# Cutting the helpers' dependent pairs in two: moving small normalization and scaling operations between VectorE, GpSimd and ScalarE in a two-layer transformer kernel

## The reference

```python
# layer 0: linear attention, 8 heads of 32
xn = ln(x, ln_w, ln_b)
q = softmax(heads(xn @ Wq + bq), axis=-1)                        # over the 32 features of a head
k = softmax(heads(xn @ Wk + bk + (1 - mask) * -1e6), axis=1)     # over the tokens
v = heads((xn @ Wv + bv) * mask)
y = einsum('bnhd,bhdl->bnhl', q, einsum('bnhd,bnhl->bhdl', k, v))
scale, shift = split(silu(emb) @ W_emb + b_emb, 2)
x = x + silu(ln(y) * (1 + scale) + shift) @ W_out + b_out
# layer 1: full attention, 16 heads of 16
xn = ln(x, norm_w, norm_b)
att = softmax(einsum('bnhl,bmhl->bnmh', q, k) + (1 - mask) * -1e6, axis=2)
y = einsum('bnmh,bmhl->bnhl', att, v)
x = x + silu(ln(y) * (1 + scale) + shift) @ out_w + out_b
```

## Time and profile before

| | us | share of the span |
|---|---|---|
| median of three runs | 870.1 | |
| span of the profiled execution | 869.6 | |
| PE busy | 825.9 | 95% |
| DVE busy | 786.1 | 90% |
| POOL busy | 732.7 | 84% |
| ACT busy | 709.8 | 82% |
| PE weight loads busy | 590.2 | 68% |

### The profile page before, as it was taken

The page is one execution under the profiler, slowest core; times in us unless marked ns, Lnnn a source line. Parts: engine busy times, 40 slices in busy tenths (PEclk is TensorE's granted clock), DMA queues, the critical chain, the costliest instruction groups (busy, mean ns, idle before and its releaser), DMA issues.

```text
span 869.6 us, 25205 instructions
## 1 busy us (share of the span) xinstructions
PE 825.9 (95%) x8653; PEld 590.2 (68%) x8653; DVE 786.1 (90%) x1610; ACT 709.8 (82%) x1250; POOL 732.7 (84%) x1214
## 2 busy tenths in 40 slices
PE   9998788999999999999999999999999999999885
PEld 4487666677777777777677777777777776656443
DVE  6898899999999999999999999999998999998962
ACT  6457847897889798888888888888888788998794
POOL 6769999799999989989999999988998887887314
PEclk8899989999999999999999999999999999999998
DMA  8221464435352525343534434334453333444311
GB/s 224 77 38 40 118 109 103 105 76 116 98 134 56 143 76 105 90 121 100 125 97 82 132 86 111 91 103 114 85 130 106 78 84 85 112 123 103 103 31 37
DMA packets 149306, 85.84 MB, mean 99 GB/s; under 512 B 87478, under 2 KB 141852, under 8 KB 149180
## 3 DMA queue, kind: packets, MB, share of 16 engines
q1 hardware_dynamic: 149180, 84.23, 39.5%
HBM read 39.52 MB, written 25.79 MB: 75 GB/s over the span
## 4 chain that ended last, share of the span: by engine, by line
PE 47%; POOL 18%; DVE 15%; issue 10%; ACT 4%; DMA 3%; SPq 2%; POOLq 0%; DVEq 0%; ACTq 0%
PE banks L690 12%; PE banks L837 7%; DVE NM L1274 6%; PE banks L698 5%; PE banks L824 4%; PE banks L813 4%; PE banks L705 3%; POOL Z L1933 2%; PE banks L720 2%; POOL ZHL L1940 2%; PE banks L847 2%; DVE st L1175 2%; POOL AB L2004 2%; PE banks L756 2%; POOL ZHL L1937 2%
## 5 line engine op out<-in xcount | busy, mean ns | idle before, releaser
L1274 DVE TENSOR_REDUCE NM<-banks 128x4 f32<-128x1024 f32 x256 | 302.5, 1212 | 9.5 <-PE banks L813 8.4
L1696 ACT ACTIVATE wraw<-banks,uu 128x1024 f32<-128x1024 f32 x154 | 170.2, 1136 | 22.3 <-PE banks L824 21.4
L1696 ACT ACTIVATE PX<-banks,uu 128x1024 f32<-128x1024 f32 x102 | 113.6, 1138 | 14.5 <-PE banks L824 12.8
L690 PE MATMUL banks<-wo,SH 128*128 128x256 f16 x768 | 96.1, 277 | 7.6 <-POOL SH L1978 7.2
L1920 POOL TENSOR_TENSOR rs<-ve,nhalf 128x2 f32<-128x2 f32 x128 | 90.2, 705 | 10.6
L813 PE MATMUL banks<-SK,SQ 51*128 51x256 f16 x1024 | 88.8, 273 | 7.0 <-DVE NM L1274 3.1
L824 PE MATMUL banks<-SQ,SK 53*128 53x256 f16 x1024 | 88.4, 272 | 6.9 <-DVE NM L1274 2.0
L690 PE MATMUL banks<-wv,ZT 128*128 128x256 f16 x768 | 94.5, 273 | 0.3 <-DVE AT L1224 0.2
L1978 POOL TENSOR_TENSOR SH<-ST,SH 128x512 f16<-128x512 f32 x64 | 74.3, 1168 | 22.9 <-ACT SH L1664 22.9
L690 PEld LDWEIGHTS banks<-wo,SH 128*128 128x128 f16 x768 | 73.2, 99 | 24.4 <-POOL SH L1978 10.5
L1678 ACT ACTIVATE R<-banks,fcs,sqs 128x256 f32<-128x256 f32 x128 | 73.8, 577 | 19.4 <-PE banks L698 19.2
(11 more groups left out here) (187 smaller groups left out, 1925.2 us busy)
## 6 DMA issues: line engine op xcount, KB each, us to landing
scr<-AB SPq DMA_DIRECT2D x64, 256.0 KB, 2.5
X<-in_x_dram SPq DMA_DIRECT2D x32, 256.0 KB, 2.9
SQ<-scr SPq DMA_DIRECT2D x64, 128.0 KB, 2.7
SK<-scr SPq DMA_DIRECT2D x64, 128.0 KB, 2.8
out_dram<-wemb SPq DMA_DIRECT2D x32, 256.0 KB, 2.5
SQ<-scr SPq DMA_DIRECT2D x64, 64.0 KB, 2.8
SK<-scr SPq DMA_DIRECT2D x64, 64.0 KB, 2.8
wemb<-in_L_cond_emb_w_dram SPq DMA_DIRECT2D x1, 1024.0 KB, 5.3
```

Source lines behind the costliest of these rows:

```text
L690: m = PE.matmul(dst[:, t, :], zt[:, j, k, t * P:(t + 1) * P], w[:, i, k, :], start=(k, n) == (0, 0), stop=(k, n) == (1, 2))
L1274: V.tensor_reduce(NMe[:, c, :, 2 * g:2 * g + 2], banks[:, n:n + 2, :].rearrange("p a (h m) -> p a h m", m=T), AX.X, ALU.max, negate=True). ...
L1696: A.activation(px(v % 5), banks[:, n:n + 2, :].rearrange("p a n -> p (a n)"), ACT.Exp, scale=uu[:, 0:1]).then_inc(S["exp"])
```

## The change

The code of five pieces and a helper is cut, and three operations change their engine:

- `stats` keeps BN_STATS; BN_AGGR is a piece of its own on DVE, `a0` to `a3`.
- `nm` and `ve` are made on ScalarE (pieces `n0` to `n3`, two ACTIVATE of 128x2); `ve` has two buffers, and epsilon comes from a tile `epa`. `norm` on POOL keeps only the power.
- `parts` on POOL is three pieces: `c0`/`c1` (Z, now one pair of buffers for each layer), `h0`/`h1` (the high part) and `z0`/`z1` (the rest).
- `km` keeps the reduction on DVE, into a new tile `kmr`; its scaling is the piece `kn` on POOL.
- `rq` is `qd` (the sum) and `rq` (the reciprocal), `Y1_` is `rd_` and `Y1_`, both on DVE.
- Of `np_` the first half is the piece `nh` on POOL, the second stays on DVE.
- `mb3` and `mh3`, used in the setup, lie in PX2.
- The order lists of all five engines and the tables of PSUM banks are new throughout.

```diff
             def stats(b, l, src):
-                e.wait_ge(S[f"s{l}"], b)
+                e.wait_ge(S[f"a{l}"], b)
                 for t in range(2):
                     i = V.bn_stats(st[:, l, t, :], src[:, t, :])
-                follow(i)
+                i.then_inc(S[f"s{l}"])
+
+            def moments(b, l):
+
+                e.wait_ge(S[f"s{l}"], b + 1)
+                e.wait_ge(S[f"n{l}"], up(b - 1))
                 for t in range(2):
                     i = V.bn_aggr(mv[:, b % 2, l, t, :], st[:, l, t, :])
-                i.then_inc(S[f"s{l}"])
+                i.then_inc(S[f"a{l}"])
...
             def km(b):
                 e.wait_ge(S["k0"], b + 1)
-                e.wait_ge(S["ke"], b)
-                follow(V.tensor_reduce(kmx[:, :], bank(home("gk0", b)), AX.X, ALU.max, negate=True))
-                V.tensor_scalar(kmx[:, :], kmx[:, :], un[:, 1:2], None, ALU.mult).then_inc(S["km"])
+                e.wait_ge(S["kn"], b)
+                V.tensor_reduce(kmr[:, :], bank(home("gk0", b)), AX.X, ALU.max, negate=True).then_inc(S["km"])
...
             def np_(b):
-                e.wait_ge(S["max"], 8 * b + 8)
-                if b == 0:
-                    ready(e, "nmz")
-                else:
-                    e.wait_ge(d_nt[(b - 1) % 2], 16 * ((b - 1) // 2 + 1))
-                follow(V.tensor_scalar(NMp[:, :, 0, :], NM[:, :, :], 2.0 ** -15, None, ALU.mult))
+                e.wait_ge(S["nh"], b + 1)
                 V.scalar_tensor_tensor(out=NMp[:, :, 1, :], in0=NM[:, :, :], scalar=2.0 ** -15, in1=NMp[:, :, 0, :],
                                        op0=ALU.mult, op1=ALU.subtract).then_inc(S["np"])
...
         @block.scalar
         def _(e):
+            def mean_of(b, l):
+                k, a = l % 2, (ZS ** -2, 1.0)[l % 2]
+                e.wait_ge(S[f"a{l}"], b + 1)
+                e.wait_ge(S[("c0", "yn0", "c1", "yn1")[l]], up(b - 1))
+                first(e, b, "cst")
+                A.activation(nm[:, b % 2, l, :], mv[:, b % 2, l, :, 0], ACT.Copy, scale=-1.0)
+                A.activation(ve[:, b % 2, l, :], mv[:, b % 2, l, :, 1], ACT.Identity, bias=epa[:, k:k + 1],
+                             scale=a).then_inc(S[f"n{l}"])
...
             def norm(b, l):
 
-                a = (1.0, ZS ** -2)[l % 2 == 0]
-                e.wait_ge(S[f"r{l}"], b)
-                G.tensor_scalar(nm[:, b % 2, l, :], mv[:, b % 2, l, :, 0], -1.0, 0.0, ALU.mult, ALU.add)
-                follow(G.tensor_scalar(ve[:, l, :], mv[:, b % 2, l, :, 1], a, EPS * a, ALU.mult, ALU.add))
-                G.tensor_tensor(rs[:, b % 2, l, :], ve[:, l, :], nhalf[:, :], ALU.pow).then_inc(S[f"r{l}"])
+                e.wait_ge(S[f"n{l}"], b + 1)
+                e.wait_ge(S[("c0", "yn0", "c1", "yn1")[l]], up(b - 1))
+                G.tensor_tensor(rs[:, b % 2, l, :], ve[:, b % 2, l, :], nhalf[:, :], ALU.pow).then_inc(S[f"r{l}"])
...
+            def kn(b):
+                first(e, b, "w0p")
+                e.wait_ge(S["km"], b + 1)
+                e.wait_ge(S["ke"], b)
+                G.tensor_scalar(kmx[:, :], kmr[:, :], un[:, 1:2], 1.0, ALU.mult, ALU.mult).then_inc(S["kn"])
+
+            def nh(b):
+                e.wait_ge(S["max"], 8 * b + 8)
+                if b == 0:
+                    ready(e, "nmz")
+                else:
+                    e.wait_ge(d_nt[(b - 1) % 2], 16 * ((b - 1) // 2 + 1))
+                G.tensor_scalar(NMp[:, :, 0, :], NM[:, :, :], 2.0 ** -15, 1.0, ALU.mult, ALU.mult).then_inc(S["nh"])
...
-            cst(); r0(0); r0(1); z0(0); xb0(0); xb0(1); z0(1); pb(); pd(); r0(2); r0(3); z0(2); r0(4); nmz()
+            nmz(); cst(); r0(0); c0(0); r0(1); xb0(0); h0(0); z0(0); xb0(1); c0(1); h0(1); v1z(); r0(2); pb()
```

More of the change, by code:

```diff
@@ new lines @@
+    "gt_f0": "0",
+    "gv0": "46774347475362375043566521644326",
+    "ga_f0": "0",
+    "gbb2": "1",
+    "gkt": "24421567564736100556121060526771",
+    "gqt": "63666246647202446535500465360633",
+    "gat": "26442553076275567624414317153465",
+    "gy0": "26434727742675112073374333472601",
+    "grw": "5",
+    "gy0T": "43275242062527252124720722610466",
+    "gcol": "5",
+    "go0": "72376515371077472233160736640061",
+    "gt_b": "0",
+    "ga_o1": "1",
+    "gt_f1": "3",
+    "ga_b": "0",
@@ L108 @@
-    "gv0": (
-        "f1m ke:1 q1:2 q1:4 mx_b th0:3 max:9 kt:7 exp:6 Y1:2 th1:2 qa:7 x1:9 max:56 max:64 exp:61 q1:17 th0:15 "
-        "th0:16 x1:16 qt:20 x1:18 th0:20 th0:21 x1:21 x1:22 th0:24 max:168 max:176 x1:26 exp:182 ka:27 "),
+    "ghot": "-",
+    "gt_w0": "-",
+    "gcnd": "hot",
+    "gpm": "-",
+    "gt_w1": "-",
+    "gt_o0": "-",
+    "ga_w0": "mx_w0",
+    "grow3": "-",
+    "ga_o0": "mx_o0",
+    "gbb0": "mc",
+    "ga_w1": "pa",
+    "gbb1": "mx_w1",
+    "gfx0": "o0p",
+    "gt_o1": "w1p",
@@ new lines @@
+    "gfx1": "bc0",
+    "gfm0": "fy0",
+    "gq0": (
+        "bc1 v:1 ke:2 qt:2 mx_b qt:5 max:6 qa:3 yt:3 vt:5 th1:2 exp:33 vt:8 vt:9 exp:56 yt:31 th0:14 exp:80 "
+        "exp:88 vt:15 max:116 vt:17 Y1:29 vt:19 th0:22 vt:21 th1:18 yt:79 Y1:41 max:188 vt:26 th0:29 "),
+    "gk0": (
+        "w0p q1:1 mx_o1 Y0:1 o1p bm+fcs max:6 vt:3 exp:10 q1:10 q1:11 yt:15 q1:13 q1:14 q1:15 yt:32 q1:17 "
+        "q1:18 q1:19 q1:20 exp:106 q1:22 q1:23 q1:24 q1:25 th0:23 th0:24 q1:28 q1:29 Y1:44 exp:185 q1:32 "),
@@ new lines @@
+    "gfm1": "fy1",
+    "gt_f0": "csT",
+    "gv0": (
+        "f0m qt:1 - x1:1 at:4 ka:1 max:8 q1:8 exp:11 ke:10 exp:27 max:47 exp:42 o:5 ka:11 exp:67 exp:75 "
+        "max:96 max:103 qt:19 max:119 o:13 exp:125 ka:20 ke:25 yt:71 q1:27 exp:164 o:20 o:21 yt:91 max:208 "),
+    "ga_f0": "mx_f0",
+    "gbb2": "ke:1",
+    "gkt": (
+        "f1m q1:2 th0:1 ke:4 ke:5 ke:6 vt:2 v:8 x1:6 ka:6 qt:10 ka:8 ke:13 qa:10 o:6 exp:69 exp:77 exp:83 "
+        "max:103 exp:99 exp:108 ka:18 at:22 qt:23 x1:22 x1:23 qt:26 o:19 x1:26 max:191 o:22 ka:28 "),
@@ L1925, in apply, with centred @@
                 i.then_inc(S[s])
[L1927 to L1938 removed]
+            def centred(b, l, src):
+                e.wait_ge(S[f"r{2 * l}"], b + 1)
+                e.wait_ge(S[f"z{l}"], b)
+                apply(b, 2 * l, Z[:, l], src, f"c{l}")
```

1045 lines of the change are left out of this document (545 added, 500 removed), and 215 rows, old and new, of the table FREED.

## The result

The changed kernel takes 857.7 us (median of 4 runs, 856.7 to 862.4) against 870.3 for the kernel before: ratio 0.986, 95% interval 0.983 to 0.989. The forecast was 861.0.

The account below looks back on a forecast made before the run. PE was taken as the bound in the middle, DVE close behind, with POOL full in the ramp. From 870.1 us the terms -5 - 4 - 2.4 + 2 = -9.4 gave 860.7, so 861 us; range 848 to 880 (8 in 10).

Parts of the forecast that it names:

- Ramp, -5: From 60 to 140 us, nm and ve leaving a full POOL saves 5 us, bounds 0 and -9.
- Cost on ScalarE, 0.43 us a pair, 464 us in the middle: nm and ve take 0.17 and 0.26 us on ScalarE, raising its busy time from 429.4 to 464 of 500 us.
- km scale and np: Moving the km scale and np's first half to POOL takes DVE from 475 to 459.5 us, POOL to 431.
- Self-waits, nothing; bound 9.8 us off the path: Self-waits becoming waits between pieces counts nothing; at most 9.8 us of DVE time, off PE's path.
- PE's order, -2.4: Switches between kinds of matmul on PE: pv in 79 blocks instead of 101 saves 2.4 us, upper bound 0.
- Middle, -4: From 200 to 700 us, DVE's relief against ScalarE's load saves 4 us of PE's waits, bounds +11 and -12.
- Tail, +2: From 700 us on, n2 and n3 added to a busy ACT cost 2 us, bounds 0 and +5.
- Head, 0: In the first 60 us, the new order of loads and setup matmuls changes nothing, bounds -3 and +3.
- Rival A: The feeders' relief stays idle on the feeders, as PE is already busy in the middle: 868.7 us, chance 0.16.
- Rival B: ScalarE becomes the engine waited for, decided once the n's wait over 0.44 us each: 881 us, chance 0.22.
- Rival C: np's second half on DVE is held while POOL's next instruction runs, undoing DVE's gain: 865.7 us, chance 0.08.
- Rival D: A large gain: ramp 9 us, middle 12, switches 2.4, head 3, tail 0, giving 843.7 us, chance 0.08.

Follow-up runs that it names:

- nm_on_gpsimd: The changed kernel with nm and ve made on GpSimd again, all else and the order as changed: 874.5 us, ratio 1.004 to the kernel before.
- scale_and_np_on_dve: The changed kernel with the km scale and first half of np on VectorE again, each behind a self-wait: 868.2 us, ratio 0.994 to the kernel before.
- old_code_new_order: The changed kernel's order, loads and banks with every edit of the code taken back: 905.9 us, ratio 1.0404 to the kernel before.
- n_twice: The changed kernel with two more ACTIVATEs, their results unread, in each n piece on ScalarE: 869.2 us, ratio 0.9949 to the kernel before.

## Why the prediction came out right, step by step

The time came out 3.3 us (0.4%) below the forecast. Two steps were wrong by more than that, with opposite signs: the tail by 10 us and the head by 5. That the sum still came so close is luck. The sum had -5 for the ramp (measured -6.1), -6.4 for middle and switches (-4.2, or -6.7 weighed by kind), +2 for the tail (-8.1) and 0 for the head (+5.4). And each edit is worth more than the sum gave it, since the new order costs much without them.

1. *Ramp, -5.* Right in size: 66 more matmuls from 60 to 200 us, 6.1 us, of which nm_on_gpsimd gives 2.5 to nm and ve. PE's wait for SH is gone from this stage. But PE's idle time from 60 to 140 fell by 1.4 us and not by some 4, and the wait for KE is still 1.8. Some 2.2 us are the clock's, which the sum had no term for: it fell behind PE's waits before (0.96 on average) and does not now (1.00).
2. *Cost on ScalarE, 0.43 us a pair, 464 us in the middle.* The term was too large. The single durations are longer than I took (0.22 and 0.30), but neighbours overlap: 0.26 a pair over the run, 455.8 in the middle and 743 in all instead of 765. The estimate from the Trainium skill ("ScalarE: Activation LUTs", section "What ACT_TABLE_LOAD costs"), where neighbours overlap by some 93 ns, was 0.28, and the trace agrees with it (0.28 at 32.01 us). I chose the larger number from rows of long instructions.
3. *km scale and np.* VectorE's middle was forecast at 459.5 and is 458.9. POOL's was forecast at 431 and is 442.5: more pieces pass in the same 500 us (YN 84 against 80, V 42 against 40), and some take longer, rs 721 ns against 699 and the second ZHL 728 against 679. kn takes 301 ns and nh 218 against 225 for each. scale_and_np_on_dve prices the edit at 7 us, 6.9 of it in the middle, so by PE's waits for NM VectorE was on PE's path in the middle.
4. *Self-waits, nothing; bound 9.8 us off the path.* Wrong. This is the step that failed most: joining the halves costs 20 to 31 us, and VectorE's alone 9.5, moved pieces included. I had priced the 34 ns of a self-wait on VectorE and left out GpSimd's c, h and z, and what the other work between the halves is worth to those who wait for it.
5. *PE's order, -2.4.* Not isolated. The order can't be had alone: with the old code it costs 35 us.
6. *Middle, -4.* Right in size, 46 matmuls or 4.2 us (6.7 weighed by kind). But the edits taken back one by one lose 8.4, 6.9 and 6.4 us in this stage, 22 in all, so the net 4 is what is left of a large gain and a large loss.
7. *Tail, +2.* Wrong sign: 8.1 us won. I saw ScalarE full in the last 170 us and took added work there as added time. In fact ScalarE had been waiting there too, mostly for PE (of its longest waits 4.6 us before YT and 6.9 before exp from 700 on; now 0.9 and 1.4): it is busy 97.0 of 100 us from 700 to 800 now (88.5 before) and PE 98.7 (96.6). Of PE's own waits from 700 on, the one for SH fell from 4.2 to 2.2 us, the one for YN stayed (2.4 and 2.5). The tail needs both order and code: from 700 on, nm_on_gpsimd is 3.7 us slower than the changed kernel by the same reckoning (1770 matmuls in 171.6 us), old_code_new_order 6.2 (2096 in 204.1).
8. *Head, 0.* Wrong: 59 matmuls fewer by 60 us, 5.4 us lost, at a granted clock of 0.86 against 0.91. The step looked only for what an earlier load could give, since PE was busy 58.56 of 60 us; it did not ask what a new setup order could lose. It lost 3.9 us of PE's waits for mxw and mxd and 2 us by the clock.

*Rival A* (PE has it already): no, the feeders' relief reached PE. *Rival B* (ScalarE waited for): no; PE's waits for ScalarE's exp and YT do not appear among its longest, and the condition (n waiting over 0.44 us each) was far off: 24.8 us of idle before nm over 128 pieces is 0.19. ScalarE is no free engine all the same: n_twice puts the price of added load near 0.25 us of time for each us. And waiting in order, the mechanism of this rival, is what the old order shows: GpSimd behind ve, ScalarE behind km. *Rival C* (np held): no, np's mean fell from 467 to 385 ns. KE's new wait, for km on GpSimd, is 1.0 us in the middle. *Rival D* (843.7): no.

## What to carry to other kernels

Where each engine works through a list in order, an edit and the order are one thing: here an edit that is worth 16 us in lists drawn for it cost 15 in lists drawn without it. So do not reject a moved instruction because it loses in the old order, nor a new order because it loses with the old code. Expect that a piece moved by a place or two in tuned lists can lose as well: VectorE's second halves moved up cost 9.5 us. In the forecast, relief of an engine is a gain only if the lists let the next piece start earlier; if they are not drawn again, look for the queue that the moved piece now waits in. And price a new setup order too: look for PE's first idle stretch, and for how long the granted clock stays low behind it.
